# A Mamba block and a mixture of experts over 16 sequences: late weights behind the first spreads, four high parts on VectorE, pair sums on GpSimd in the last sequence, and new written orders at both ends

## The chip, the cores and the metric

The kernel runs on one core of a Trainium2 chip. The metric is the device time of one execution in microseconds. The same code also runs once under the hardware profiler, and all rows below are from that execution. The engines are called PE (matrix multiplication), DVE (VectorE), ACT (ScalarE), POOL (GpSimd) and SP (SyncE, which here only issues DMAs). Each works through its own list of instructions in order and waits for the others at semaphores.

## The reference, cut to what matters

The input `x` is 16 sequences of 512 tokens with 128 channels, in fp32. Two residual blocks follow each other:

```python
x = x + attn(layernorm(x))          # a selective scan, 256 inner channels, 16 states
x = x + ffn(layernorm(x))           # 8 experts, the best 2 of each token, and one shared expert

# attn
x_proj, z = split(x @ W_in + b_in)
u = silu(x_proj)
B, C = split(u @ W_xproj + b_xproj)            # 16 values each per token
dt = softplus(u @ W_dt + b_dt)
# for each token t, channel d, state s:
h[d, s] = h[d, s] * exp(dt[t, d] * A[d, s]) + dt[t, d] * u[t, d] * B[t, s]
y[t, d] = sum over s of h[d, s] * C[t, s] + D[d] * u[t, d]
out = (y * silu(z)) @ W_out + b_out

# ffn
h = silu(x @ w1.T) * (x @ w3.T);  out_e = h @ w2.T        # for each of the 9 experts
out = sum over e of out_e * weight[e] + shared
```

## The kernel before

One sequence is one unit of work. Its 512 tokens lie along the free dimension, and the 256 inner channels are two halves `c` of 128 partitions. A *step* `a` is one half and one state, so there are 32 steps to a sequence, 0 to 15 for the first half. The names in the orders are tasks, `name.argument+sequence`:

- `x_t`, `xp`, `z`, `bc`, `dl` (PE) transpose and project the normalised input; `x_tc`, `u`, `zs`, `bcc`, `dlc` (ACT) take the results out of PSUM. `dlc` gives `dt`, `bcc` the rows of B and C.
- `rows` and `spread` (SP) write B and C to DRAM and read them back, copied to all 128 partitions, into `b_all` and `c_all`, in four groups of four states. In the first sequence `bs` and `cs` issue B and C of a group apart. Each is 1024 KB.
- `w` makes `dt * u`. `dbu` (POOL, line 785) multiplies it by B for four steps at once. `decay` (ACT, line 689) makes exp(dt * A) of a step in one of two PSUM banks.
- `scan` (DVE, line 902) runs the recurrence of a step over 512 tokens. For the steps in `by_dve(m)` it writes back into PSUM, and `mul` (DVE, line 910) multiplies by C into `hc`. For all others it writes to `hc`, and `hcp` (POOL, line 795) multiplies two neighbours by C in place. `hc` has four slots, `dbu` eight.
- `red` (PE, line 1079) adds one step to `y_acc`: four transposing matmuls, which free the slot in `hc`. `ycopy`, `gy`, `gyc`, `proj`, `projc` finish the first block.
- `mom2`, `agg2`, `rs2`, `norm2`, `split`, `splitc`, `xhi`, `xlo` normalise the result and split it into a high and a low part. `route`, `routec`, `rexp`, `rank` choose the experts. `h1` and `h3` (PE, line 989, three matmuls for each of 18 units, two units to an expert), `silu` (ACT), `g` (DVE), `eo` (PE, line 996, the output of one expert), `sc` (ACT) and `comb` (DVE) do the second block. `shared` is the shared expert's output. `store` writes the sequence.
- `whi` and `wlo` split the nine expert weights into high and low parts once, at the start. `late` is six weight transfers (w_out, b_out, w2 of 1152 KB, the gate's weights and bias, a constant `below`) which `resb.0` (POOL, line 764), `proj.0` and later tasks wait for.

The order of each engine is written out by hand in three parts: `START` covers the beginning, `ORDER` is one window that is repeated with the sequence number going up by one, and `END` is the last stretch. The block of the experts lags the scan by two to three sequences. The two PSUM banks of `mixed` and the three of `h` are given out in the order of the PE list (`InTurn`), so a move of a PE task changes who waits for whom.

```python
START_TO, END_FROM = 3, SEQS - 1 - 1      # windows 4 to 13 are repeated, END covers the rest
```

In front of window 4 START has brought POOL to `w.0` of sequence 5. END has the rest of sequence 14 and all of 15.

Of the kernel before, what the change touches and what calls it, by code (L numbers as in the profile page):

```python
# [58 lines left out]
def by_pool(m):  # L59
# [51 lines left out]
        red.13+1 dl.0+2 dl.1+2 route.0 h1.2 red.14+1 red.15+1 h1.3 gy.0+1 red.16+1 h1.4 h1.5 red.17+1
        red.18+1 h1.6 red.19+1 bc.0+2 h3.2 eo.0 red.20+1 h3.3 red.21+1 red.22+1 h1.7 red.23+1 h1.8 h3.4
        red.24+1 red.25+1 eo.1 red.26+1 h3.5 red.27+1 red.28+1 red.29+1 h3.6 red.30+1 h1.9 red.31+1 gy.1+1
        eo.2 red.0+2 proj.0+1 z.0+2 h1.10 h1.11 red.1+2 red.2+2 z.1+2 h3.7 red.3+2 x_t.0+3 red.4+2 h1.12
        red.5+2 red.6+2 h3.8 eo.3 red.7+2 h3.9 xp.0+3 h1.13 red.8+2 red.9+2 h1.14 h3.10 h3.11 red.10+2
# [1038 lines left out]
```

## Time and profile before

| | us |
|---|---|
| runs (3) | 1208.53 median, 1208.41 to 1209.28 |
| profiled execution | 1208.65 |
| its span | 1206.8 |
| PE, DVE, ACT, POOL busy | 1125.5, 1092.8, 1091.0, 1048.5 |

The span runs from the first to the last instruction, and 1.85 us of the execution lie around it. Busy time is the time in which at least one instruction of an engine runs. The ends of matmuls are modelled, so PE can be shown busy over short gaps: how long a piece of PE work really takes is read from the distance between starts in the chain.

### The profile page before, as it was taken

How to read it: one execution, taken by the hardware profiler on the slowest of the kernel's cores; microseconds unless marked ns; L12 is line 12 of the kernel's file. 1: busy time of each engine (PE TensorE's matmuls, PEld its weight loads, DVE VectorE, ACT ScalarE, POOL GpSimd, SP SyncE). 2: the span in 40 equal slices, each digit the busy share in tenths (PEclk: the TensorE clock that was granted, in tenths of full speed). 3: DMA queues.
4: the chain of work that ended last, by engine and by line, in shares of the span. 5: the costliest groups of instructions: out<-in, count | busy, mean ns of one | idle time of the engine just before them, and what ended most of it. 6: DMA issues, size and time to landing. Idle time of an engine off the chain costs nothing.

```text
span 1206.8 us, 21930 instructions
## 1 busy us (share of the span) xinstructions
PE 1125.5 (93%) x7352; PEld 949.5 (79%) x7352; DVE 1092.8 (91%) x1666; ACT 1091.0 (90%) x1916; POOL 1048.5 (87%) x459
## 2 busy tenths in 40 slices
...
GB/s 239 223 209 82 142 157 117 183 38 262 19 282 24 203 100 82 219 18 281 27 212 88 127 182 12 288 18 250 50 163 146 64 236 10 182 118 1 19 9 10
DMA packets 49456, 153.68 MB, mean 127 GB/s; under 512 B 4416, under 2 KB 31424, under 8 KB 32832
## 3 DMA queue, kind: packets, MB, share of 16 engines
...
q8 instruction: 59, 0.97, 0.3%
...
## 4 chain that ended last, share of the span: by engine, by line
POOL 45%; PE 27%; issue 15%; ACT 6%; DVE 4%; DMA 1%; SPq 1%; POOLq 0%; DVEq 0%; ACTq 0%
POOL dbu L785 23%; POOL hc L795 18%; PE h L989 12%; PE mixed L996 8%; PE y_acc L1079 4%; DVE hc L902 2%; ACT da L689 2%; POOL res L764 1%; POOL w_s L772 1%; ACT L689 1%; DMA below<-in_below 1%; POOL rstd L756 1%; DVE g L951 1%; PE mixed L989 1%; ACT silu L723 1%
## 5 line engine op out<-in xcount | busy, mean ns | idle before, releaser
L785 POOL TENSOR_TENSOR dbu<-w_s,b_all 128x2048 f32<-128x2048 f32 x128 | 585.8, 4577 | 19.9 <-DMA b_all<-bc_rows 19.9
L795 POOL TENSOR_TENSOR hc<-hc,c_all 128x1024 f32<-128x1024 f32 x151 | 359.2, 2382 | 51.7 <-DVE hc L902 51.2
L689 ACT ACTIVATE da<-dt_s,a_neg 128x512 f32<-128x512 f32 x512 | 346.0, 691 | 46.6 <-DVE hc L902 24.1
L902 DVE TENSOR_TENSOR_SCAN hc<-da,dbu 128x512 f32<-128x512 f32 x302 | 358.5, 1211 | 22.8 <-PE y_acc L1079 11.6
L1079 PE MATMUL y_acc<-ident,hc 128*128 128x128 f32 x2048 | 297.6, 282 | 43.3 <-POOL hc L795 30.7
L1079 PEld LDWEIGHTS y_acc<-ident,hc 128*128 128x128 f32 x2048 | 248.8, 145 | 97.8 <-POOL hc L795 41.1
L996 PEld LDWEIGHTS mixed<-w_s,g 128*128 128x128 f32 x2304 | 273.4, 193 | 26.0 <-DVE g L951 13.2
L996 PE MATMUL mixed<-w_s,g 128*128 128x128 f32 x2304 | 285.2, 277 | 8.9 <-DVE g L951 6.3
L902 DVE TENSOR_TENSOR_SCAN da<-da,dbu 128x512 f32<-128x512 f32 x210 | 252.7, 1218 | 16.0 <-POOL dbu L785 10.3
L989 PE MATMUL h<-x_hi,w_hi 128*128 128x512 f32 x576 | 257.5, 447 | 5.8 <-DVE g L951 4.3
L989 PE MATMUL h<-x_lo,w_hi 128*128 128x512 f32 x576 | 227.9, 396 | 0.0
L989 PE MATMUL h<-x_hi,w_lo 128*128 128x512 f32 x576 | 227.7, 395 | 0.0
L951 DVE TENSOR_TENSOR g<-silu,h 128x512 f32<-128x512 f32 x288 | 193.3, 676 | 28.2 <-PE h L989 14.4
L723 ACT ACTIVATE silu<-h 128x512 f32<-128x512 f32 x288 | 160.8, 602 | 13.9 <-PE h L989 9.9
L730 ACT ACTIVATE mixed<-mixed,comb 128x128 f32<-128x128 f32 x512 | 140.9, 339 | 23.3 <-PE mixed L996 18.6
L910 DVE TENSOR_TENSOR hc<-da,c_all 128x512 f32<-128x512 f32 x210 | 140.7, 680 | 5.8 <-PE y_acc L1079 4.8
L689 ACT ACT_TABLE_LOAD x111 | 142.4, 1283 | 2.0
L989 PEld LDWEIGHTS h<-x_hi,w_hi 128*128 128x128 f32 x576 | 109.2, 189 | 31.0 <-DVE g L951 8.2
L989 PEld LDWEIGHTS h<-x_hi,w_lo 128*128 128x128 f32 x576 | 108.5, 188 | 25.6
L989 PEld LDWEIGHTS h<-x_lo,w_hi 128*128 128x128 f32 x576 | 109.6, 190 | 9.9 <-issue 0.2
L723 ACT ACT_TABLE_LOAD x79 | 101.4, 1283 | 1.4
L959 DVE TENSOR_TENSOR acc<-mixed,acc 128x512 f32<-128x512 f32 x112 | 75.5, 674 | 10.8 <-ACT mixed L730 6.2
...
## 6 DMA issues: line engine op xcount, KB each, us to landing
b_all<-bc_rows SPq DMA_DIRECT2D x64, 1024.0 KB, 6.4
c_all<-bc_rows SPq DMA_DIRECT2D x64, 1024.0 KB, 8.8
...
```

The source lines that it names most:

```text
L689: act.activation(da[a % DA_SLOTS][:, :], dt_s[:, m % DT_SLOTS, c, :], ACT.Exp, scale=a_neg[:, a:a + 1]).then_inc(decay_made, 1)
L723: act.activation(silu[:, a % SILU_SLOTS, :], h_tile("h1", a, m)[:, :], ACT.Silu).then_inc(silu_made, 1)
L730: last = act.activation(block_, block_, ACT.Copy, scale=comb[:, b, a:a + 1])
L785: pool.tensor_tensor(dbu[:, at:at + AT_ONCE, :], w_s[:, c, None, :].broadcast_to([P, AT_ONCE, T]), b_all[:, s:s + AT_ONCE, :], ALU.mult).t ...
L795: pool.tensor_tensor(pair, pair, c_all[:, s:s + 2, :], ALU.mult).then_inc(c_by_pool, 1)
L902: dve.tensor_tensor_scan(dst, ring[:, :], dbu[:, a % DBU_SLOTS, :], 0.0, ALU.mult, ALU.add).then_inc(scanned, 1)
L910: dve.tensor_tensor(hc[:, a % HC_SLOTS, :], da[a % DA_SLOTS][:, :], c_all[:, s, :], ALU.mult).then_inc(c_by_dve, 1)
L951: dve.tensor_tensor(g[:, a % G_SLOTS, :], silu[:, a % SILU_SLOTS, :], h_tile("h3", a, m)[:, :], ALU.mult).then_inc(g_made, 1)
L959: dve.tensor_tensor(acc[:, :, :], as_blocks(tile), acc[:, :, :], ALU.add).then_inc(freed, 1)
L989: last = pe.matmul(dst[:, :], w, xx[:, :], start=(i == 0), stop=(i == 2))
L996: last = pe.matmul(as_blocks(tile)[:, b, :], g[:, slot, b * P:(b + 1) * P], w2_s[:, at:at + DM], start=(begins and b == 0 and f == 0), sto ...
L1079: last = pe.matmul(y_acc[:, b, :], hc[:, a % HC_SLOTS, b * P:(b + 1) * P], ident[:, :], is_transpose=True, start=(a % NS == 0 and b == 0), ...
```

## The change

1. SP, start: the late weights are issued behind all spreads of the first sequence, and B of groups 2 and 3 comes earlier. `loadres` of sequences 0 and 1 is moved too.
2. The high parts of the expert weights 1, 3, 5 and 7 are made on DVE instead of ACT. `w.1` of the first sequence is moved ahead of its scans.
3. `resb.0` on POOL goes from between `dbu.1` and `dbu.2` of the first sequence to behind `dbu.0` of the second. `dl.1` goes ahead of `z.1`, and `dlc.1` ahead of the first decays.
4. In the last sequence POOL adds each pair of products (`padd`, 16 times 128x512), and PE reduces only the sum: 16 `red` instead of 32. A `scan` or `mul` then waits for the reduction where its slot was an even one and for the add where it was an odd one (`hc_free`).
5. START and END are written anew for all engines, and END begins one window earlier, so it covers the rest of sequence 13 and all of 14 and 15. `ORDER` is unchanged.
6. Functions for "turned" steps come with it (`turned`, tasks `bt`, `wt`, `td`, `tb`, `btc`, `wtc`). Their list is empty and no order holds these tasks, so they issue nothing.

```diff
+HI_BY_DVE = [1,3,5,7]
+TURNED_FIRST = []
+PAIRED = 1
+def in_pairs(m):
+    return m >= SEQS - PAIRED
+def sums(m):
+    return range(0, STEPS, 2) if in_pairs(m) else range(STEPS)
+def sum_count(step, m):
+    return sum(len(sums(k)) for k in range(m)) + len([a for a in sums(m) if a <= step])
+def pair_count(step, m):
+    return STEPS // 2 * (m - (SEQS - PAIRED)) + step // 2 + 1
...
-START_TO, END_FROM = 3, SEQS - 1 - 1
+START_TO, END_FROM = 3, SEQS - 1 - 2
```

START on PE, first entries:

```diff
-        x_t.0 xp.0 xp.1 bc.0 dl.0 z.0 z.1 dl.1 red.0 red.1 red.2 red.3 x_t.0+1 red.4 red.5 red.6 red.7 red.8
+        x_t.0 xp.0 xp.1 bc.0 dl.0 z.0 dl.1 z.1 x_t.0+1 red.0 red.1 red.2 red.3 red.4 red.5 red.6 red.7
```

START on ACT, first entries:

```diff
-        aexp.0 x_tc.0 u.0 u.1 whi.0 whi.1 bcc.0 whi.2 whi.3 whi.4 whi.5 whi.6 whi.7 dlc.0 whi.8 decay.0
-        decay.1 zs.0 zs.1 dlc.1 decay.2 decay.3 decay.4 norm1.0+1 decay.5 decay.6 decay.7 decay.8 decay.9
+        aexp.0 x_tc.0 u.0 u.1 whi.0 bcc.0 dlc.0 whi.2 whi.4 dlc.1 zs.0 whi.6 decay.0 decay.1 whi.8 zs.1
+        decay.2 norm1.0+1 decay.3 x_tc.0+1 decay.4 decay.5 decay.6 decay.7 decay.8 decay.9 decay.10 decay.11
```

START on DVE, first entries and the place of `comb.0`:

```diff
-        mom1.0 agg1.0 winlo.0 norm1.0 x_lo.0 wlo.0 wlo.1 wlo.2 wlo.3 mom1.0+1 wlo.4 wlo.5 wlo.6 wlo.7
-        agg1.0+1 w.0 wlo.8 scan.0 mul.0 scan.1 mul.1 scan.2 mul.2 scan.3 mul.3 scan.4 mul.4 scan.5 mul.5
-        scan.6 scan.7 scan.8 mul.8 scan.9 mul.9 scan.10 scan.11 x_lo.0+1 w.1 scan.12 mul.12 scan.13 mul.13
+        mom1.0 agg1.0 winlo.0 norm1.0 x_lo.0 whi.1 whi.3 w.0 wlo.0 wlo.1 wlo.2 wlo.3 whi.5 mom1.0+1 agg1.0+1
+        wlo.4 whi.7 w.1 wlo.5 wlo.6 wlo.7 wlo.8 scan.0 mul.0 scan.1 mul.1 scan.2 mul.2 scan.3 mul.3 scan.4
+        mul.4 scan.5 mul.5 scan.6 scan.7 scan.8 scan.9 mul.8 mul.9 scan.10 scan.11 x_lo.0+1 scan.12 mul.12
...
-        scan.28+1 scan.29+1 mul.28+1 mul.29+1 comb.0 g.5 scan.30+1 scan.31+1 mul.30+1 mul.31+1 comb.1
+        mul.21+1 rank.7 scan.22+1 scan.23+1 comb.0 scan.24+1 scan.25+1 mul.24+1 mul.25+1 g.3 g.4 scan.26+1
```

START on POOL, first entries:

```diff
-        rs1.0 dbu.0 dbu.1 rs1.0+1 resb.0 dbu.2 hcp.6 dbu.3 hcp.10 dbu.4 hcp.14 dbu.5 hcp.18 dbu.6 hcp.22
-        dbu.7 w.0+1 hcp.26 dbu.0+1 rs1.0+2 dbu.1+1 hcp.2+1 dbu.2+1 rs2.0 hcp.6+1 dbu.3+1 w.1+1 hcp.10+1
+        rs1.0 dbu.0 rs1.0+1 dbu.1 dbu.2 hcp.6 dbu.3 hcp.10 dbu.4 hcp.14 dbu.5 hcp.18 dbu.6 hcp.22 dbu.7
+        w.0+1 hcp.26 dbu.0+1 rs1.0+2 resb.0 dbu.1+1 hcp.2+1 dbu.2+1 rs2.0 hcp.6+1 dbu.3+1 w.1+1 hcp.10+1
```

START on SP, first entries:

```diff
-        load.0 raw.0 load.0+1 rows.0 bs.0 bs.1 cs.0 loadres.0 late.0 cs.1 bs.2 cs.2 cs.3 bs.3 load.0+2
-        rows.0+1 spread.0+1 spread.1+1 spread.2+1 spread.3+1 load.0+3 rows.0+2 spread.0+2 spread.1+2
-        spread.2+2 loadres.0+1 spread.3+2 load.0+4 rows.0+3 spread.0+3 spread.1+3 spread.2+3 spread.3+3
+        load.0 raw.0 load.0+1 rows.0 bs.0 bs.1 cs.0 bs.2 cs.1 bs.3 cs.2 load.0+2 loadres.0 cs.3 late.0
+        rows.0+1 spread.0+1 spread.1+1 spread.2+1 spread.3+1 load.0+3 rows.0+2 loadres.0+1 spread.0+2
+        spread.1+2 spread.2+2 spread.3+2 load.0+4 rows.0+3 spread.0+3 spread.1+3 spread.2+3 spread.3+3
```

END on PE, from the first experts of sequence 13 to the first of sequence 15:

```diff
-        red.25-1 route.0-2 h1.0-2 red.26-1 h1.1-2 red.27-1 h1.2-2 red.28-1 h1.3-2 h3.0-2 h1.4-2 red.29-1
-        h1.5-2 shared.0-3 h1.6-2 h3.1-2 h3.2-2 red.30-1 red.31-1 h1.7-2 h3.3-2 eo.0-2 red.0 red.1 h1.8-2
-        h1.9-2 h3.4-2 h3.5-2 eo.1-2 red.2 red.3 h3.6-2 h3.7-2 eo.2-2 h1.10-2 gy.1-1 red.4 h1.11-2 red.5
...
-        h1.10-1 h3.8-1 red.26 h1.11-1 red.27 eo.3-1 h3.9-1 h1.12-1 red.28 z.1 h3.10-1 red.29 red.30 red.31
-        h1.13-1 h3.11-1 gy.1 eo.4-1 proj.0 h3.12-1 eo.5-1 h1.14-1 h3.13-1 h3.14-1 h1.15-1 eo.6-1 h1.16-1
-        h3.15-1 h1.17-1 split.0 h3.16-1 h3.17-1 eo.7-1 h1.0 h1.1 h3.0 route.0 shared.0-1 h1.2 h3.1 h3.2 h1.3
+        h1.17-3 h3.17-3 red.25-1 eo.7-3 h1.0-2 red.26-1 red.27-1 route.0-2 h3.0-2 h1.1-2 h1.2-2 h1.3-2
+        red.28-1 shared.0-3 red.29-1 h1.4-2 h1.5-2 h3.1-2 h3.2-2 red.30-1 red.31-1 h3.3-2 eo.0-2 h3.4-2
+        h1.6-2 eo.1-2 h3.5-2 red.0 h1.7-2 h1.8-2 red.2 h3.6-2 gy.1-1 eo.2-2 h3.7-2 h1.9-2 red.4 h3.8-2
+        proj.0-1 h3.9-2 eo.3-2 red.6 h1.10-2 h1.11-2 h1.12-2 eo.4-2 h1.13-2 h1.14-2 h1.15-2 h3.10-2 h3.11-2
+        h3.12-2 red.8 eo.5-2 h3.13-2 red.10 eo.6-2 h3.14-2 h1.16-2 z.0 h3.15-2 h1.17-2 split.0-1 red.12
...
+        h3.5-1 h3.6-1 red.22 red.24 eo.2-1 h3.7-1 h1.10-1 h3.8-1 h3.9-1 eo.3-1 h3.10-1 h1.11-1 red.26
+        h1.12-1 eo.4-1 h1.13-1 red.28 h1.14-1 z.1 h3.11-1 h3.12-1 red.30 h1.15-1 gy.1 h3.13-1 proj.0 eo.5-1
+        h3.14-1 h1.16-1 h3.15-1 eo.6-1 h3.16-1 split.0 h1.17-1 h3.17-1 eo.7-1 h1.0 route.0 h1.1 h3.0
```

END on DVE, the first steps of sequence 15 (new order only):

```diff
+        scan.31-1 rank.0-2 scan.0 rank.1-2 scan.1 rank.2-2 mul.0 rank.3-2 rank.4-2 rank.5-2 comb.7-3
+        rank.6-2 mul.1 g.1-2 g.2-2 scan.2 scan.3 rank.7-2 g.3-2 g.4-2 scan.4 comb.0-2 scan.5 g.5-2 mul.4
```

END on POOL, whole:

```diff
-        hcp.26-1 hcp.28-1 dbu.0 hcp.30-1 dbu.1 hcp.2 dbu.2 w.1 hcp.6 resb.0-1 dbu.3 hcp.10 dbu.4 rs2.0-1
-        hcp.12 hcp.14 dbu.5 hcp.18 dbu.6 hcp.22 dbu.7 hcp.26 hcp.28 resb.0 hcp.30 rs2.0
+        hcp.26-2 dbu.0-1 hcp.28-2 hcp.30-2 dbu.1-1 w.1-1 hcp.2-1 dbu.2-1 rs1.0 hcp.6-1 dbu.3-1 resb.0-2
+        hcp.10-1 dbu.4-1 hcp.12-1 hcp.14-1 dbu.5-1 hcp.18-1 dbu.6-1 rs2.0-2 hcp.22-1 dbu.7-1 w.0 hcp.26-1
+        dbu.0 hcp.28-1 hcp.30-1 w.1 dbu.1 padd.0 hcp.2 padd.2 dbu.2 padd.4 resb.0-1 hcp.6 padd.6 dbu.3
+        padd.8 hcp.10 rs2.0-1 padd.10 dbu.4 hcp.12 padd.12 hcp.14 padd.14 dbu.5 padd.16 hcp.18 padd.18 dbu.6
+        padd.20 hcp.22 padd.22 padd.24 dbu.7 hcp.26 padd.26 hcp.28 padd.28 hcp.30 padd.30 resb.0 rs2.0
```

The tasks:

```diff
+        def hc_free(a, m):
+            user, back = before(a, HC_SLOTS, STEPS)
+            if m < back:
+                return reduced, 0
+            if in_pairs(m - back) and user % 2:
+                return pair_added, pair_count(user, m - back)
+            return reduced, sum_count(user, m - back)
...
+                elif what == "whi":
+                    dve.wait_ge(raw_in[a // RAW], 16 * RAW)
+                    dve.tensor_copy(w13_hi[:, a * W13:(a + 1) * W13], stages[a]).then_inc(hi_by_dve, 1)
...
+                elif what == "padd":
+                    pool.wait_ge(*c_count(a + 1, m))
+                    at = a % HC_SLOTS
+                    pool.tensor_tensor(hc[:, at, :], hc[:, at, :], hc[:, at + 1, :], ALU.add).then_inc(pair_added, 1)
...
-                    pe.wait_ge(*c_count(a, m))
+                    if in_pairs(m):
+                        pe.wait_ge(pair_added, pair_count(a, m))
+                    else:
+                        pe.wait_ge(*c_count(a, m))
```

## Rows read from the trace of the kernel before

**Rows 1.** Profile page: busy time of all engines, costliest groups, DMA issues.
```profile
PE 1125.5 (93%) x7352; PEld 949.5 (79%) x7352; DVE 1092.8 (91%) x1666; ACT 1091.0 (90%) x1916; POOL 1048.5 (87%) x459
...
L795 POOL TENSOR_TENSOR hc<-hc,c_all 128x1024 f32<-128x1024 f32 x151 | 359.2, 2382 | 51.7 <-DVE hc L902 51.2
...
b_all<-bc_rows SPq DMA_DIRECT2D x64, 1024.0 KB, 6.4
```

**Rows 2.** Stretches: length, busy PE, PEld, DVE, ACT, POOL (count), clock, DMA share, GB/s.
```profile
0.00:50.00 50.00, 27.43 (x135) 19.01 (x136) 28.86 (x51) 29.61 (x44) 23.02 (x20) 0.74 0.76 279
50.00:100.00 50.00, 31.32 (x171) 25.02 (x169) 45.74 (x58) 35.45 (x49) 49.49 (x19) 0.81 0.42 170
...
600.00:700.00 100.00, 98.55 (x654) 82.50 (x653) 95.44 (x143) 97.60 (x176) 96.32 (x43) 1.00 0.41 157
...
1100.00:1150.00 50.00, 50.00 (x333) 44.13 (x332) 39.46 (x66) 38.40 (x75) 25.08 (x12) 1.00 0.04 12
```

**Rows 3.** Timeline of POOL: start, duration, instruction, idle before; one of sequence 14.
```profile
966.36 1.29 POOL L772 TENSOR_TENSOR w_s<-dt_s,u 128x512 f32<-128x512 f32 x1
```

**Rows 4.** Timeline of SP, which issues DMAs, first 30 us.
```profile
18.73 0.81 SPq L606 DMA_DIRECT2D b_all<-bc_rows  x2
...
21.76 0.44 SPq L588 DMA_DIRECT2D w_s<-in_w  x1
...
26.66 0.42 SPq L606 DMA_DIRECT2D b_all<-bc_rows  x1
```

**Rows 5.** Timeline of POOL in the first 60 us.
```profile
23.70 8.98 POOL L785 TENSOR_TENSOR dbu<-w_s,b_all 128x2048 f32<-128x2048 f32 x2 [15.79 <-DMA b_all<-bc_rows]
32.77 0.23 POOL L744 TENSOR_SCALAR minus_mean<-moments 128x4 f32<-128x4 f32 x1
...
36.19 1.27 POOL L764 TENSOR_TENSOR res<-res,bout_s 128x512 f32<-128x512 f32 x1 [1.48 <-DMA below<-in_below]
40.84 4.51 POOL L785 TENSOR_TENSOR dbu<-w_s,b_all 128x2048 f32<-128x2048 f32 x1 [3.38 <-DMA b_all<-bc_rows]
...
55.60 4.52 POOL L785 TENSOR_TENSOR dbu<-w_s,b_all 128x2048 f32<-128x2048 f32 x1
```

**Rows 6.** Timeline of DVE and, last row, of ACT in the first 50 us.
```profile
28.31 1.23 DVE L902 TENSOR_TENSOR_SCAN da<-da,dbu 128x512 f32<-128x512 f32 x1 [5.78 <-POOL dbu L785]
29.58 0.69 DVE L910 TENSOR_TENSOR hc<-da,c_all 128x512 f32<-128x512 f32 x1
...
34.29 1.23 DVE L902 TENSOR_TENSOR_SCAN da<-da,dbu 128x512 f32<-128x512 f32 x1 [2.16 <-ACT da L689]
...
41.75 2.33 DVE L902 TENSOR_TENSOR_SCAN hc<-da,dbu 128x512 f32<-128x512 f32 x2
45.45 1.23 DVE L902 TENSOR_TENSOR_SCAN da<-da,dbu 128x512 f32<-128x512 f32 x1 [1.37 <-POOL dbu L785]
...
31.57 0.69 ACT L667 ACTIVATE dt_s<-mixed,bdt_s 128x512 f32<-128x512 f32 x1
```

**Rows 7.** Timelines of SP and POOL: the `res` of sequence 1.
```profile
148.22 0.38 SPq L556 DMA_DIRECT2D res<-in_x  x1
...
158.32 1.27 POOL L764 TENSOR_TENSOR res<-res,bout_s 128x512 f32<-128x512 f32 x1 [1.36 <-DMA res<-in_x]
```

**Rows 8.** The chain that ended last: start, duration, piece; sequence 15.
```profile
1064.51 0.87 PE y_acc L1079 x8
1065.38 2.80 PE h L989 x12
1068.18 1.78 PE mixed L996 x16
...
1138.41 1.31 PE y_acc L1079 x12
...
1158.12 2.23 PE h L989 x9
```

**Rows 9.** Waits of POOL between 1052 and 1138 us: total, times, longest.
```profile
POOL hc L795 <- DVE hc L902: 18.2, 8, 5.5
```

**Rows 10.** Timeline of PE between 60 and 100 us.
```profile
84.27 5.33 PE L1079 MATMUL y_acc<-ident,hc 128*128 128x128 f32 x24 [4.68 <-POOL hc L795]
```

More of the change, by code:

```diff
@@ L52, with turned, dbu_count, turned_count @@
 ]
+TURNED_FIRST = []
+def turned(m):
+    return TURNED_FIRST[m] if m < len(TURNED_FIRST) else []
+def dbu_count(step, m):
+    own = [g for g in range(step // AT_ONCE + 1) if g not in turned(m)]
+    return sum(DBUS - len(turned(k)) for k in range(m)) + len(own)
+def turned_count(step, m):
+    own = [a for a in range(step + 1) if a // AT_ONCE in turned(m)]
+    return AT_ONCE * sum(len(turned(k)) for k in range(m)) + len(own)
+PAIRED = 1
[7 more added lines that the diff above has]
+    return STEPS // 2 * (m - (SEQS - PAIRED)) + step // 2 + 1
 def by_dve(m):
@@ L111 @@
[L111 to L115, printed above, removed]
@@ L178 @@
[L178 removed]
+        rs1.0 dbu.0 rs1.0+1 dbu.1 dbu.2 hcp.6 dbu.3 hcp.10 dbu.4 hcp.14 dbu.5 hcp.18 dbu.6 hcp.22 dbu.7
+        w.0+1 hcp.26 dbu.0+1 rs1.0+2 resb.0 dbu.1+1 hcp.2+1 dbu.2+1 rs2.0 hcp.6+1 dbu.3+1 w.1+1 hcp.10+1
+        dbu.4+1 hcp.14+1 dbu.5+1 hcp.18+1 dbu.6+1 hcp.22+1 dbu.7+1 hcp.26+1 w.0+2 dbu.0+2 dbu.1+2 rs1.0+3
+        w.1+2 resb.0+1 hcp.2+2 dbu.2+2 hcp.6+2 dbu.3+2 hcp.10+2 dbu.4+2 rs2.0+1 hcp.14+2 dbu.5+2 rs1.0+4
@@ L179 @@
+        hcp.18+2 dbu.6+2 hcp.22+2 dbu.7+2 w.0+3 hcp.26+2 dbu.0+3 hcp.30+2 dbu.1+3 hcp.2+3 w.1+3 dbu.2+3
+        hcp.6+3 dbu.3+3 resb.0+2 hcp.10+3 dbu.4+3 hcp.12+3 hcp.14+3 dbu.5+3 hcp.18+3 rs2.0+2 dbu.6+3
+        hcp.22+3 dbu.7+3 w.0+4 hcp.26+3 dbu.0+4 hcp.28+3 hcp.30+3 dbu.1+4 hcp.2+4 w.1+4 dbu.2+4 rs1.0+5
+        hcp.6+4 dbu.3+4 resb.0+3 hcp.10+4 dbu.4+4 hcp.12+4 hcp.14+4 dbu.5+4 rs2.0+3 hcp.18+4 dbu.6+4
         hcp.22+4 dbu.7+4 w.0+5
@@ L776, in task @@
                     c, s = step // NS, step % NS
-                    if s == 0:
+                    if not [g for g in range(c * NS // AT_ONCE, a) if g not in turned(m)]:
                         pool.wait_ge(w_made, NC * m + c + 1)
```

376 lines of the change are left out of this document (223 added, 153 removed).

## The prediction

> **What bounds the kernel now.** I read the page's first part [rows 1], then the busy time by stretch [rows 2], then the timelines of both ends, because those are what the change touches. In the middle PE is busy 98.6 of 100 us and POOL, ACT and DVE 96 to 98 of 100 [rows 2]: one sequence takes 69.4 us (POOL starts `w.0` of sequence 14 at 966.36, and this row recurs every 69.4 us, nine times from 342.02 on [rows 3]) and no engine has room. That stretch keeps its order, so what is gained before it is carried through it, and the question is what the two ends do. In the first 50 us POOL works 23 and DVE 29; in 1100 to 1150 PE is full and POOL works 25.1 [rows 2]. The start is therefore bound by data that arrives late and by the step loop of the first sequence, the end by PE.
>
> **First sequence, DMA order.** SP issues the first two B spreads at 18.73, then one C spread, then the late weights (`w2` at 21.76, 1152 KB), and only at 26.66 the B spread of group 2 (group 3 at 28.22, a row of the same form) [rows 4]. POOL ends `rs1` at 34.7, waits 1.48 us for the last late weight, does `resb.0` (1.27), waits 3.38 more for group 2 and starts `dbu.2` at 40.84 [rows 5]. The first spread lands at 23.70; from there to group 2's landing at 40.84 are 17.1 us for 5.7 MB (four spreads, `res`, the late weights), 3.0 us each [rows 4, 5]. With the late weights last, group 2 is the third megabyte behind the first and lands at 23.7 + 9 = 32.7. It stops being what `dbu.2` waits for; that is then scan 3, whose results free the slots. The old order also let DVE wait 2.16 us at 34.29 for a decay that stood on ACT behind `dlc.1`, done at 32.26 [rows 6]; the new one has PE do `dl.1` before `z.1` and ACT `dlc.1` before the decays, with `bc.0` and `dl.0` as early as before. Scan 0 stays where it is, 28.1 to 28.3: `dbu.0` waits for the first spread, not for DVE or ACT. Steps of scan and product take 1.87 us (34.29 to 41.75 for four), two bare scans 2.33 [rows 6]. Scan 3 ends at 28.2 + 3 x 1.87 + 1.2 = 35.0, `dbu.2` runs 35.0 to 39.5 (rs1, 2 us, and `dbu.1` are done at 34.7). Scan 7 ends at 28.2 + 6 x 1.87 + 2.34 = 41.8, where before scan 8 started at 45.45, behind `dbu.2`. `hcp.6` 41.8 to 44.1, `dbu.3` 44.1 to 48.6, `hcp.10` to 50.95, and `dbu.4` starts at 50.95 instead of 55.60 [rows 5]: **-4.65**.
>
> What moves with it: the four high parts on DVE. No row has an fp32 copy on DVE; below stands nothing, above 0.69 of a two-input operation of that size [rows 6]. I take 0.6, 2.4 in all, and cost it at nothing: before, DVE sat idle 5.78 us in front of scan 0 [rows 6]. If ACT's `whi.8` slips past 27, scan 0 slips with it, 0 to 1.5 us; that end is kept for the range. `w.1` moves from behind scan 11 to before scan 0, into the same idle. `resb.0` goes behind `dbu.0+1`, where POOL has no wait: **+1.25** [rows 5]. `loadres.0+1` now goes ahead of the spreads of sequence 2 instead of behind three of them: its `res` was issued at 148.22 and POOL waited 1.36 us for it at 158.32 [rows 7]: **-1.3**. It adds a wait: SP holds the next sequence's spreads until `comb.0` is done. In the new DVE order `comb.0` stands behind scan 23 instead of behind the product of step 29, and B has then 9 to 10 us of POOL work (`hcp.22`, `dbu.7`, `hcp.26`, `w.0`) to arrive in; a B spread's median is 6.4 [rows 1]. Nothing, or up to 3 us if it misses. The other moves in sequences 1 to 3 change places of equal work; POOL, DVE and ACT each wait some 5 us in 100 to 200, so I bound them by -3 and +3 and take 0. Start: **-4.7**.
>
> **Sequences 13 to 15, PE.** One h unit (three matmuls) is 0.70 us of the chain, one expert output 1.78, one reduction 0.44 [rows 8]. In the old order 12 h units and one output of sequence 13 are done when `red.0` of sequence 15 comes, in the new one 13 units and two outputs. The chain is PE there, so it comes **+2.5** later.
>
> **The last sequence.** Sixteen reductions go: 16 x 0.44 = 7.0 us of PE. Sixteen adds come to POOL. Nearest rows: POOL's `w` and `resb`, 512 elements with two inputs, 1.29 and 1.27 [rows 3, 5]; the lower bound is half a 1024-element product, 1.19 [rows 1], the upper 1.29. An operation of POOL starts some 0.03 to 0.05 before the one ahead of it ends in its row, so I take 1.25, 20.0 in all. From the first add to the last POOL has in its new order 6 `dbu` at 4.53, 10 products (`hcp`) at 2.33, 15 adds, one `resb`, one `rs2` (1.98): 27.2 + 23.3 + 18.8 + 1.25 + 2.0 = 72.5 us. Walking the orders against each other I find 2.7 us of waits: `hcp.2` for scan 3 behind two `g` (1.3), and about 1.4 at `red.8` and `red.26`, which the new order puts behind 8 us of PE work each while slots wait. 75.2, against 74.8 from the end of `red.0` (1064.95) to the end of `red.31` (1139.72) [rows 8]. So the adds go into POOL's waits (18.2 us in 1052 to 1138 [rows 9]) nearly whole, and the stretch stays: **+0.4**. But PE, which was its bound, is now idle in it by some 6 us and PE's saving is not the end's.
>
> The Trainium skill speaks against this step: the page "GPSIMD Engine Reference", section "4.1 Engine selection", sends elementwise adds on a tile to VectorE, GpSimd being about twice as slow. The trace agrees: 0.69 for a product on DVE against 1.19, half of 2.38, on POOL [rows 1, 6]. The page's figure for an add of 2048 fp32 elements, 4497 ns, would make an estimate of 1.12 each and 18.0 in all, and the end 2 us earlier.
>
> **The tail.** From `red.31` (1139.72) to h1.0 of the last sequence (1158.12) are 18.4 us [rows 8]. The bare durations of that path, each from its row in the timeline (ycopy 0.60, gy 0.44, gyc 0.69, proj 1.79, projc 0.69, bn_stats 0.87, aggregate 0.38, rs2 1.95, norm2 1.65, split 0.44, copy and high part 1.2, low part 0.69, and 14 handovers near 0.1) sum to 13; the rest is h units and outputs of sequence 14 standing ahead of it on PE. In the new order four units and one output of these are done before the last reduction, and 13.4 us of PE work are left ahead of h1.0. Between 13 and 18.4 I take 15: **-3.4**. Behind h1.0 nothing changes: 36 units, nine outputs, the last add and the store, 48.7 us.
>
> **Sum**, against the profiled execution of 1208.65 (span 1206.8 and 1.85 around it; the median of the runs, 1208.53, is 0.1 lower): -4.7 + 2.5 + 0.4 - 3.4 = -5.2, so **1203.4 us**.
>
> **Rivals.** (B) *PE stays the bound to the end.* If the new order of sequences 13 and 14 lets POOL start the last sequence earlier than PE work alone says, the last stretch ends with PE: the start's 4.7 and 7.0 of reductions, 1208.65 - 11.7 = **1197.0**. For it: the chain is PE without a gap from 1060 to 1200 [rows 8]; against: POOL's 72.5 us of work between first and last add, which no order shortens. (C) *The start's gain is given back* in sequences 1 to 3, because DVE is full from 50 us on (45.7 of 50 [rows 2]) and the spreads of sequence 2 now stand behind `comb.0`; or the late weights were hidden anyway behind scan 3. Then -0.5 is left, **1208.2**. Against: DVE's idle time in the first 50 us is what shrinks, and it counts like POOL's. (D) *The adds on POOL end late*, the case on the other side. Place: between `padd.0` and `padd.30`; price: every microsecond of the 18.2 us of waits that stays beside the 20.0 of adds [rows 9]. These waits are for scans, which wait for reductions to free slots, and the slot now comes free one operation later (product, add, reduction). My walk leaves 2.7; from 7.7 more on it is slower than before by over 0.2%; with 10 more **1213.4**. (E) *PE's clock falls in the new gaps.* Granted clock is 1.00 where no gap of PE is over half a microsecond and 0.81 in 50 to 100 us, where it waits 3.5 to 4.7 us between reductions; there 24 matmuls of a reduction take 5.33 us, twice the 2.6 of six at the end [rows 2, 8, 10]. My walk has one gap of 3.1 us before `red.2` and a few in the tail. If about 10 us of PE work on the path run at the 1.2 GHz level, that is +5: **1208.4**. The Trainium skill, "TensorE: Matmul & The Clock Gate", section "Part 1: The HAM clock gate", says likewise that idling brings the slower level back and activity releases it; the trace agrees with that. That the change doesn't do what it says has one form: the functions for turned steps come with it, but their list is empty, so they issue nothing.
>
> **Chances.** Forecast 0.48 (own range 1200 to 1206.5), B 0.20, C 0.15, D 0.10, E 0.07. What a measurement can tell from no change is 0.2%, 2.4 us. Faster than 1206.1: nearly all of the forecast (0.46), B, and a little of C and E: 0.67. Within 0.2%: 0.22. Slower: D and a remainder of the reordering that I bounded by +3: 0.11. The range of 8 in 10 takes in most of B and C and leaves D out: 1196 to 1209.5.
>
> **What would show it.** Start: `dbu.2` at about 35, `dbu.4` at about 51, `w.0` of sequence 4 near 268 (272.65 before), and no wait of POOL before a `res` add. C is right if that `w.0` is later than 271. End: PE idle several microseconds between the first and last reduction of sequence 15, and POOL busy in over 70 of some 75 us there; B if PE is without gaps, D if POOL waits over 10 us there, E if the granted clock is under 0.97 in any stretch behind 1050. The tail from the last reduction to the end of the span: 63.7 against 67.1. The forecast is wrong if the last reduction does not end near 1138, or if the tail stays at 67.

## The result and the profile after

The changed kernel takes 1207.66 us (median of 12 runs, 1204.9 to 1210.15), the kernel before 1209.75 (12 runs beside it, 1206.96 to 1212.33): ratio 0.9981, 95% interval 0.9972 to 0.9990. That is 2.3 us faster, where 5.2 were forecast. Its profiled execution spans 1206.4 us, against 1206.8.

The page of the changed kernel, and its stretches (columns as in [rows 2]):

```profile
PE 1123.4 (93%) x7288; PEld 944.6 (78%) x7288; DVE 1098.6 (91%) x1670; ACT 1090.9 (90%) x1914; POOL 1069.9 (89%) x475
```

```profile
0.00:50.00 50.00, 24.89 (x126) 17.75 (x127) 33.52 (x55) 26.46 (x38) 22.57 (x19) 0.72 0.76 276
50.00:100.00 50.00, 34.22 (x161) 26.69 (x160) 43.39 (x55) 36.59 (x50) 48.65 (x19) 0.67 0.43 173
...
1050.00:1100.00 50.00, 49.40 (x328) 43.54 (x327) 47.06 (x75) 47.94 (x90) 49.44 (x24) 1.00 0.34 124
1100.00:1150.00 50.00, 49.19 (x311) 41.57 (x310) 41.46 (x68) 43.46 (x78) 42.05 (x21) 1.00 0.04 12
```

POOL has 21 us more work (16 adds), TensorE 64 matmuls less. In the first 50 us DVE is *busier* by 4.7 us than before [rows 2], yet what came to it is 1.7 us of copies and `w.1` (0.7): something took longer. DVE's timeline of the changed kernel shows what:

```profile
20.75 0.69 DVE L1004 TENSOR_TENSOR w_s<-dt_s,u 128x512 f32<-128x512 f32 x1 [7.46 <-ACT dt_s L765]
21.36 2.49 DVE L991 TENSOR_TENSOR w_lo<-silu,w_hi 128x512 fp32r<-128x512 f32 x4
23.76 4.74 DVE L984 CAST w_hi<-silu 128x512 fp32r<-128x512 f32 x1
...
30.30 0.42 DVE L984 CAST w_hi<-g 128x512 fp32r<-128x512 f32 x1
30.64 0.69 DVE L1004 TENSOR_TENSOR w_s<-dt_s,u 128x512 f32<-128x512 f32 x1
...
31.84 1.89 DVE L991 TENSOR_TENSOR w_lo<-g,w_hi 128x512 fp32r<-128x512 f32 x3
33.66 1.22 DVE L1041 TENSOR_TENSOR_SCAN da<-da,dbu 128x512 f32<-128x512 f32 x1
```

The third high part takes 4.74 us, eleven times the fourth (0.42), and scan 0 starts at 33.66, 5.4 us later than before [rows 6]. POOL in the same stretch:

```profile
23.17 5.06 POOL L907 TENSOR_TENSOR dbu<-w_s,b_all 128x2048 f32<-128x2048 f32 x1 [15.54 <-DMA b_all<-bc_rows]
30.01 0.76 POOL L864 TENSOR_SCALAR minus_mean<-moments 128x4 f32<-128x4 f32 x1 [1.78 <-DVE moments L1025]
...
33.15 4.95 POOL L907 TENSOR_TENSOR dbu<-w_s,b_all 128x2048 f32<-128x2048 f32 x1
40.61 4.52 POOL L907 TENSOR_TENSOR dbu<-w_s,b_all 128x2048 f32<-128x2048 f32 x1 [2.51 <-DVE da L1041]
```

`dbu.0` runs from 23.17 to 28.23, the long high part from 23.76 to 28.50: it ends 0.3 us behind POOL's operation. `dbu.2` starts at 40.61 (forecast 35; 40.84 in [rows 5]), though it no longer waits for its spread but for scan 3. Where POOL starts sequence 4, and the ends of the last sequence (first and last add on POOL, then first and last reduction on PE):

```profile
278.34 1.29 POOL L894 TENSOR_TENSOR w_s<-dt_s,u 128x512 f32<-128x512 f32 x1
...
1066.21 1.30 POOL L923 TENSOR_TENSOR hc<-hc 128x512 f32<-128x512 f32 x1
...
1141.45 1.29 POOL L923 TENSOR_TENSOR hc<-hc 128x512 f32<-128x512 f32 x1
```

```profile
1070.97 0.60 PE L1231 MATMUL y_acc<-ident,hc 128*128 128x128 f32 x4
...
1142.80 0.66 PE L1231 MATMUL y_acc<-ident,hc 128*128 128x128 f32 x4
```

Four marks cut every profile into the forecast's terms: POOL's first `w` of sequence 4 (`w.0`), the start of `red.0` of sequence 15, the end of the last reduction, the end of the span. In us, with three kernels that are told below:

```
                       before   changed   e3       e11      e7
to w.0 of seq. 4       272.65   278.34    272.99   272.69   270.24
from there to red.0    791.69   792.63    792.93   792.78   792.62
red.0 to last red      75.38    72.49     72.54    76.92    72.57
last red to the end    67.08    62.94     62.94    62.91    62.87
```

Changed against before: +5.7, +0.9, -2.9, -4.1, in sum -0.4. Forecast: -4.7, +2.5, +0.4, -3.4. The spans are those of one profile each, and the first row moves most from one execution to the next: with the old start it lies between 272.65 and 272.99 in four profiles (before, e3, e11, e14), with the new one at 278.34 here and at 274.41 in e4.

### The profile page after: what moved, and what is told of

Read it like the earlier page. It is cut to its first block, busy times and chain, and to the rows that moved or that the text cites. A ratio compares the mean times of both kernels' runs of the same rounds, so it can differ in the third digit from the quotient of the medians.

```text
span 1206.4 us, 21820 instructions
## 1 busy us (share of the span) xinstructions
PE 1123.4 (93%) x7288; PEld 944.6 (78%) x7288; DVE 1098.6 (91%) x1670; ACT 1090.9 (90%) x1914; POOL 1069.9 (89%) x475
## 4 chain that ended last, share of the span: by engine, by line
POOL 47%; PE 22%; issue 16%; DVE 8%; ACT 7%; DMA 1%; DVEq 0%; POOLq 0%; ACTq 0%; SPq 0%
POOL dbu L907 23%; POOL hc L917 19%; PE h L1127 9%; PE mixed L1134 6%; PE y_acc L1231 4%; DVE hc L1041 4%; ACT da L810 2%; ACT L810 1%; POOL w_s L894 1%; POOL hc L923 1%; POOL res L884 1%; POOL rstd L876 1%; ACT silu L843 1%; DVE da L1041 1%; PE mixed L1198 1%
## 5 line engine op out<-in xcount | busy, mean ns | idle before, releaser
L1231 PE MATMUL y_acc<-ident,hc 128*128 128x128 f32 x1984 | 289.8, 282 | 36.3 <-POOL hc L917 23.3
L1231 PEld LDWEIGHTS y_acc<-ident,hc 128*128 128x128 f32 x1984 | 240.8, 145 | 93.6 <-POOL hc L917 37.2
```

The lines of the kernel that those rows point to most:

```text
L1231: last = pe.matmul(y_acc[:, b, :], hc[:, a % HC_SLOTS, b * P:(b + 1) * P], ident[:, :], is_transpose=True, start=(a % NS == 0 and b == 0), ...
```

## Experiments

All but e10 were timed in alternation with the kernel before, in three groups on one chip: e1 to e4; e7, e8, e9 and e11; e12, e13 and e14. e10 ran once, beside the last group. A ratio is to the kernel before, and a ratio times 1209.5 gives the microseconds.

**e3 and e4: one half of the change each.** e3 has `START_ORDER` of before and `HI_BY_DVE = []` in the changed kernel, e4 `END_ORDER`, `END_FROM` of before and `PAIRED = 0`.

```diff
-HI_BY_DVE = [1,3,5,7]
+HI_BY_DVE = []
```

> The first four windows in the order of the kernel before, all high parts on ScalarE; the last windows and the pair adds of the changed kernel. Theory (the new first part costs 5.7 us, the new last part gains 8): w.0 of sequence 4 at 272.6, the last sequence as in the changed kernel but 5.7 us earlier, about 1202.0 us, 7.8 below the kernel before. Rival 1 (the last part only gains because it takes back what the start lost, so that PE or GpSimd work sets its end): 1205 us or more. Rival 2 (as forecast, the last part is worth 0.5 us): 1209.

> The first windows of the changed kernel with its high parts on VectorE; the last windows and all 32 reductions of the kernel before. Theory: the start's loss of 5.7 us is carried to the end, 1209.75 + 5.7 = 1215.4 us, slower than before by 0.47%. Rival 1 (the loss is taken back in the last windows, whichever their order): 1210 to 1212 us. Rival 2 (the start did gain, as forecast): 1205.

e3: 1203.21 us, ratio 0.9951 (0.9939 to 0.9963). e4: 1212.43, 1.0033 (1.0022 to 1.0043). The new last part is worth -0.49% with the old start, and -0.52% with the new one (0.9981 against 1.0033): 5.9 to 6.3 us, not the 0.5 of the forecast and, as e3 shows, nothing that the start had lost first. The new start costs 0.33% with the old end and 0.30% with the new: 3.6 to 4.0 us, where 4.7 of gain were forecast. The expected 5.7 came from one profile; in e4's the same start has `w.0` of sequence 4 at 274.41, 1.8 us behind before, and the span ends 1.7 behind (1208.5), so nothing of the loss is taken back in the last windows.

**e1 and e2: the long high part.** e1 makes the four high parts by a two-input operation, e2 puts all four ahead of `w.0`.

```diff
-dve.tensor_copy(w13_hi[:, a * W13:(a + 1) * W13], stages[a])
+dve.tensor_tensor(w13_hi[:, a * W13:(a + 1) * W13], stages[a], stages[a], ALU.max)
```

```diff
-whi.1 whi.3 w.0 wlo.0 wlo.1 wlo.2 wlo.3 whi.5 mom1.0+1 agg1.0+1 wlo.4 whi.7 w.1
+whi.1 whi.3 whi.5 whi.7 w.0 wlo.0 wlo.1 wlo.2 wlo.3 mom1.0+1 agg1.0+1 wlo.4 w.1
```

> The four high parts stay on VectorE at their places, but each is made by a two-input maximum of the tile with itself in place of a copy; the values are the same. Theory (a copy of an fp32 tile on VectorE is held for as long as a GpSimd operation runs beside it: whi.5 took 4.74 us and ended 0.27 behind dbu.0): the two-input form takes about 0.69 us each, whi.5 too, and scan 0 starts at about 29.6 instead of 33.66 (the 5.16 us of work behind whi.5 counted from 23.76 + 0.69). That lead is carried: w.0 of sequence 4 near 274.3 instead of 278.34, and about 1203.7 us against 1207.7. Rival 1 (whi.5 was late for another reason, its data or ScalarE): it still ends near 28.5, nothing changes. Rival 2 (the start is lost by the orders of sequences 1 to 3 and not by the high part): scan 0 comes earlier, but w.0 of sequence 4 stays within 1 us of 278.3 and the time within 1.5 us of 1207.7.

> whi.5 and whi.7 stand on VectorE directly behind whi.3, in its idle time of 7.5 us ahead of w.0, where GpSimd does nothing. Theory: both take 0.43 us as whi.1 and whi.3 do, scan 0 starts at about 28.5 (33.66 less 4.74 less 0.42, and dbu.0 ends at 28.2), w.0 of sequence 4 near 273.2, and 1202.5 us. Rival 1 (another reason than GpSimd holds whi.5): it is long there too and w.0 slips behind 20.75. Rival 2 (orders of sequences 1 to 3): scan 0 early, w.0 of sequence 4 still within 1 us of 278.3, time within 1.5 us of 1207.7.

e1: 1211.26, ratio 1.0021 (1.0012 to 1.0031), slower than the changed kernel. e2: 1206.68, 0.9981 (0.9971 to 0.9991), no better. My first theory, that only a copy is held, is wrong. DVE of e1:

```profile
22.53 0.68 DVE L984 TENSOR_TENSOR w_hi<-silu 128x512 fp32r<-128x512 f32 x1
...
24.44 4.07 DVE L991 TENSOR_TENSOR w_lo<-silu,w_hi 128x512 fp32r<-128x512 f32 x1
...
30.23 6.18 DVE L991 TENSOR_TENSOR w_lo<-g,w_hi 128x512 fp32r<-128x512 f32 x3
36.34 1.22 DVE L1041 TENSOR_TENSOR_SCAN da<-da,dbu 128x512 f32<-128x512 f32 x1
```

and of e2:

```profile
22.39 4.65 DVE L991 TENSOR_TENSOR w_lo<-silu,w_hi 128x512 fp32r<-128x512 f32 x1
...
29.97 1.22 DVE L1041 TENSOR_TENSOR_SCAN da<-da,dbu 128x512 f32<-128x512 f32 x1
```

Now a low part is held: whatever operation with both inputs in SBUF comes to DVE first while `dbu.0` runs (23.43 to 27.95 in e1, 21.96 to 26.49 in e2) ends 0.55 us behind it. e1 has a second one beside `dbu.1` (three low parts in 6.18 us, the last of them 4.98). e2's scan 0 is 3.7 us earlier than the changed kernel's and `w.0` of sequence 1 as well (78.67 against 82.36), yet its time is the same. In its profile the lead is still 3.2 us at `w.0` of sequence 3 (208.27 against 211.44) and gone at sequence 4 (278.54); between 210 and 220 the granted clock is 0.66 there, 1.00 in the changed kernel. But that is one of its slower executions (1209.04, median 1206.68), so why the lead is missing in the time of all twelve stays open.

**e10: the low parts alone.** The kernel before with one order edited:

```diff
-wlo.0 wlo.1 wlo.2 wlo.3 mom1.0+1 wlo.4 wlo.5 wlo.6 wlo.7 agg1.0+1 w.0 wlo.8 scan.0
+wlo.0 mom1.0+1 agg1.0+1 w.0 wlo.1 wlo.2 wlo.3 wlo.4 wlo.5 wlo.6 wlo.7 wlo.8 scan.0
```

> The kernel before with one edit: VectorE's low parts 1 to 8 stand behind w.0 and not ahead of it. Without any hold they end near 26.8, ahead of dbu.0's end at 28.2, and scan 0 stays at 28.3. Theory of the hold (two SBUF inputs on VectorE wait for a GpSimd operation under way): dbu.0 starts at 23.7, after four of them; the fifth takes about 4 us in place of 0.69 and ends with dbu.0, three more follow, and scan 0 starts at 30.1. Since scan 2 waits for its decay until 34.29 anyway, both expect the time of before, within 1 us.

One run: 1213.19 us against 1208.77 (nine runs, none above 1210.55), and `w.0` of sequence 4 at 277.27, 4.6 later. DVE of e10, then POOL:

```profile
21.81 11.70 DVE L857 TENSOR_TENSOR w_lo<-silu,w_hi 128x512 fp32r<-128x512 f32 x5
33.44 1.88 DVE L857 TENSOR_TENSOR w_lo<-g,w_hi 128x512 fp32r<-128x512 f32 x3
35.24 1.22 DVE L902 TENSOR_TENSOR_SCAN da<-da,dbu 128x512 f32<-128x512 f32 x1
```

```profile
23.47 9.50 POOL L785 TENSOR_TENSOR dbu<-w_s,b_all 128x2048 f32<-128x2048 f32 x2 [15.65 <-DMA b_all<-bc_rows]
...
42.19 4.52 POOL L785 TENSOR_TENSOR dbu<-w_s,b_all 128x2048 f32<-128x2048 f32 x1 [4.76 <-DVE da L902]
```

The first row holds five low parts. Two of these and the two `dbu`, by source line for what runs after 28 us (shortest/median/longest in ns, first and last start):

```profile
L857 DVE TENSOR_TENSOR w_lo<-silu,w_hi x2: 4981/4988/4995, 23.6 to 28.5; 128x512 fp32r<-128x512 f32 x2
L785 POOL TENSOR_TENSOR dbu<-w_s,b_all x2: 4596/4771/4946, 23.5 to 28.0; 128x2048 f32<-128x2048 f32 x2
```

Three low parts took 0.68, and the fourth and the fifth 5.0 us each: one was held beside `dbu.0`, was let through at its end, and the next one came to DVE when `dbu.1` had begun and was held for that. Each ended 0.5 us behind its `dbu`. The hold was as expected, but it came twice, and scan 0 starts at 35.24 instead of the expected 30.1, which also makes the "same time" wrong.

**e7: nothing left to be held.** The changed kernel, with DVE's low parts 0 to 7 and all high parts ahead of `w.0`, and on ACT `whi.2 whi.4 whi.6` ahead of `dlc.0` and `whi.8` ahead of `dlc.1`:

```diff
-whi.1 whi.3 w.0 wlo.0 wlo.1 wlo.2 wlo.3 whi.5 mom1.0+1 agg1.0+1 wlo.4 whi.7 w.1 wlo.5 wlo.6 wlo.7 wlo.8 scan.0
+whi.1 whi.3 wlo.0 wlo.1 whi.5 wlo.2 wlo.3 whi.7 wlo.4 wlo.5 wlo.6 wlo.7 w.0 wlo.8 mom1.0+1 agg1.0+1 w.1 scan.0
```

> The changed kernel; in its first sequence VectorE does all four high parts and the low parts 0 to 7 ahead of w.0, in its idle time, ScalarE does whi.2, 4 and 6 ahead of dlc.0, and only wlo.8, the statistics and w.1 are left between w.0 and scan 0. Theory (VectorE operations with two SBUF inputs are held for the rest of dbu.0, and all that stands behind the held one comes after it): with one or none left, scan 0 starts 0.1 to 0.7 us behind the end of dbu.0, at 26.6 to 28.6, instead of 5.4, 3.5 and 3.8 us behind it; w.0 of sequence 1 at 76.5 (82.36, 78.67 and 80.09 in the three kernels with this start), w.0 of sequence 4 at 272.5, and 1203.8 us (1207.7 less 3.9). Rival (the place of scan 0 is not what sets the first sequence; its DMAs or slots do): w.0 of sequence 1 not earlier than 78.5 and 1206.5 us or more.

1200.26 us, ratio 0.9935 (0.9913 to 0.9957): 7.9 us faster than before and 5.6 faster than the changed kernel (the two intervals lie apart), by the order of a dozen instructions. The expectation was 3.9 faster than the changed kernel, with `w.0` of sequence 4 at 272.5 and not at 270.24; the 1.7 us above it lie within the intervals. DVE and POOL of e7:

```profile
22.04 0.66 DVE L1004 TENSOR_TENSOR w_s<-dt_s,u 128x512 f32<-128x512 f32 x1
27.18 1.23 DVE L1041 TENSOR_TENSOR_SCAN da<-da,dbu 128x512 f32<-128x512 f32 x1 [4.48 <-POOL dbu L907]
```

```profile
22.42 4.65 POOL L907 TENSOR_TENSOR dbu<-w_s,b_all 128x2048 f32<-128x2048 f32 x1 [14.53 <-DMA b_all<-bc_rows]
...
34.15 4.52 POOL L907 TENSOR_TENSOR dbu<-w_s,b_all 128x2048 f32<-128x2048 f32 x1 [0.59 <-DVE da L1041]
...
49.87 4.56 POOL L907 TENSOR_TENSOR dbu<-w_s,b_all 128x2048 f32<-128x2048 f32 x1
```

Scan 0 waits for `dbu.0` and nothing else, `dbu.2` and `dbu.4` start at 34.15 and 49.87 (forecast 35 and 50.95), and `w.0` of sequence 1 at 75.91, 4.7 us ahead of before. This is the start that the prediction described, but for scan 0: it comes 1.0 us earlier than forecast, because the first spread lands earlier (`dbu.0` at 22.42, 23.70 in [rows 5]).

**e8, e9, e12: the other parts of the start**, each with the new last part. e8 is e3 with the late weights behind the last C spread and `resb.0` later:

```diff
-bs.0 bs.1 cs.0 loadres.0 late.0 cs.1 bs.2 cs.2 cs.3 bs.3 load.0+2
+bs.0 bs.1 cs.0 bs.2 cs.1 bs.3 cs.2 cs.3 loadres.0 late.0 load.0+2
```

e9 adds `dl.1` ahead of `z.1`, `dlc.1` ahead of `zs.0` and `w.1` ahead of scan 0. e12 is e9 with the high and low parts of e7 in it and `rs1` of sequence 1 ahead of `dbu.1`, as in the change; its sequences 1 to 3 keep the old order.

> The old order of the first windows with the last part of the changed kernel (1203.2 us); from the change's first sequence only the order of DMAs (late weights behind the last C spread) and resb.0 behind dbu.0 of sequence 1. Theory of the prediction: dbu.2 no longer waits for its spread but for scan 3 and starts at 37.3 instead of 39.77, dbu.4 at about 51.5 instead of 54.92, resb.0 adds 1.25 later where GpSimd is full, so w.0 of sequence 4 at 270.8 instead of 272.99 and 1201.0 us. Rival (what the spreads gain is taken back in sequences 1 to 3, whose order is the old one): 1203 us.

> The kernel of e8 with the second dt moved as in the change: dl.1 ahead of z.1, dlc.1 ahead of zs.0 and the decays, w.1 on VectorE ahead of scan 0. Scan 2 then waits for nothing (2.31 us before) unless decay.2 is later than 31.8. Theory: scan 0 at 28.5 (w.1 is held until dbu.0 ends), dbu.2 at 35.3, dbu.4 at 50.9, w.0 of sequence 4 at 270, 1200 us. Rival: w.1 beside dbu.0 and one more change of ScalarE's function in the start cost what the 2.31 us give, 1201 to 1202 us.

> The first sequence of e7 (all low parts but one and all high parts ahead of w.0, late weights last, second dt early), sequences 1 to 3 in the old order with resb.0 behind dbu.0 of sequence 1, the new last part. Between w.0 of sequence 1 and w.0 of sequence 4 the new order took 194.3 to 196.0 us (e7, e4, e1, the changed kernel), the old one 192.0 to 193.4 with resb.0 in it (before, e3, e8, e9). Theory (the new order of sequences 1 to 3 itself costs 1 to 3 us): w.0 of sequence 1 at 75.9, of sequence 4 at 269.3, and 1199.4 us against 1200.3 of e7. Rival (an earlier first sequence is swallowed in sequences 1 to 3 under either order): w.0 of sequence 4 at 270.2 or later, 1200.3 us or more.

e8: 1203.14 (0.9948, 0.9931 to 0.9964); e9: 1202.55 (0.9943, 0.9922 to 0.9962); e12: 1200.22 (0.9932, 0.9918 to 0.9946). In e8 `dbu.2` starts at 37.57 as worked out, but `dbu.4` at 53.77 (expected 51.5), `w.0` of sequence 1 at 79.75, where e11 has it with the old start, and that of sequence 4 at 272.93, as in e3: the DMA order with the moved `resb.0` is worth nothing. In e9 `w.0` of sequence 1 is at 78.48 and that of sequence 4 at 271.90 (expected 270), and its time is nearer to its rival; `w.1`, held beside `dbu.0`, took 2.81 us. e12 is no faster than e7 (`w.0` of sequence 1 at 75.31, of sequence 4 at 269.47, 194.2 us between them; 194.3 in e7, 192.0 before). The time can't tell its theory (1199.4) from its rival (1200.3), but the stretch between the marks speaks for the rival: with either order, 2 of the 4.7 to 5.3 us won in the first sequence are gone by sequence 4. The moved `resb.0` is 1.27 us of POOL's work in that stretch; e8, which has it, loses 0.6 there against e3.

**e13: the `res` load ahead of the spreads**, alone in the kernel before.

```diff
-spread.0+2 spread.1+2 spread.2+2 loadres.0+1 spread.3+2
+loadres.0+1 spread.0+2 spread.1+2 spread.2+2 spread.3+2
```

> The kernel before with one edit in SP's order: the res load of sequence 1 stands ahead of the spreads of sequence 2 instead of behind three of them. The prediction's term: GpSimd's wait of 1.36 us for it at 158.32 goes, 1.3 us earlier from there on, 1208.0 against 1209.3. Rival: the wait goes, but GpSimd then waits as long for scans or the spreads, 1209.3.

1215.11, ratio 1.0045 (1.0031 to 1.0060): both expectations wrong. SP of e13, then POOL:

```profile
146.86 0.39 SPq L556 DMA_DIRECT2D res<-in_x  x1
147.57 0.34 SPq L606 DMA_DIRECT2D b_all<-bc_rows  x1
```

```profile
152.26 4.51 POOL L785 TENSOR_TENSOR dbu<-w_s,b_all 128x2048 f32<-128x2048 f32 x1 [5.66 <-issue]
```

The load waits on SP for `comb.0` (its last operation on DVE ends at 146.76) until 146.86 and the spreads behind it start 7.9 us later than before (139.72). In the changed kernel `comb.0` stands six scans earlier in DVE's order, the load goes at 138.29 and the first spread at 139.01: there the wait has its cover, and e13 shows it gone where the SP edit stands alone. The move of `comb.0` alone was not run.

**e11 and e14: the adds.** e11 is e3 with all 32 reductions and no adds; e14 is the kernel before with the adds and 16 reductions, in the old order.

```diff
-red.0 h1.7-2 h1.8-2 red.2
+red.0 red.1 h1.7-2 h1.8-2 red.2 red.3
```

```diff
-hcp.30-1 dbu.1 hcp.2 dbu.2 w.1 hcp.6
+hcp.30-1 dbu.1 padd.0 hcp.2 padd.2 dbu.2 padd.4 w.1 hcp.6 padd.6
```

> The old start with the new order of the last windows, but all 32 reductions of the last sequence on TensorE and no adds on GpSimd: each second reduction stands right behind the first of its pair. Against 1203.2 us with the adds. Theory (TensorE is busy 49.2 to 49.4 of 50 us from 1050 to 1150 with the adds and would have to take 16 reductions of 0.44 us more): 7 us later less what is idle, 1209 us, which is about the kernel before; the gain of the last part is then that of the adds. Rival (the gain is the new order's and the adds only move work from TensorE to GpSimd, whose 20 us of adds lie in waits): 1203 to 1204 us. Rival 2 (GpSimd is the bound of the last sequence with the adds): 1198 to 1201 us.

> The kernel before with the pair adds alone: old start, old order of the last windows, in the last sequence 16 reductions and 16 adds on GpSimd behind each pair's product. Theory (adds and new order are worth their gains each by itself: e11 against e3 gave 4.0 us for the adds, e11 against before 2.1 for the order): 1205.2 us. Rival 1 (in the old order GpSimd starts the last sequence later and TensorE is the bound, so 16 reductions of 0.44 us come off in full): 1202.3. Rival 2 (the old order leaves GpSimd's waits for scans in place, 18.2 us, and the adds come on top): 1209 us or more.

e11: 1207.24, 0.9987 (0.9977 to 0.9998). e14: 1226.39, 1.0147 (1.0131 to 1.0163). In the new order the adds bring 0.36%, 4.4 us, all of it between `red.0` and the last reduction (76.9 against 72.5 us in the table). In the old order they cost 17.8 us. POOL's waits from 1050 to 1160 in e14, then those of the changed kernel from 1051 to 1144:

```profile
POOL hc L895 <- DVE hc L1020: 10.9, 2, 7.2
POOL hc L889 <- DVE hc L1013: 4.6, 3, 3.9
```

```profile
POOL hc L917 <- DVE hc L1041: 1.1, 2, 1.0
POOL hc L923 <- DVE hc L1048: 0.3, 1, 0.3
```

In e14 an add (L895) stands in POOL's queue ahead of the next `dbu` and waits up to 7.2 us for a product of DVE, in whose queue `g` operations stand ahead and wait up to 3.0 us each for TensorE's `h`; TensorE in its turn waits 15.7 us for POOL at its reductions (busy 39.8 of 50 us from 1100 on, granted clock 0.91). The prediction's rival D is real under the old order: the adds are as good as the order around them, and the theory that the two parts add up is refuted.

## Why the prediction was wrong, point by point

**The step that failed: "the four high parts on DVE", taken as 2.4 us and "cost ... at nothing", in 5.78 us of idle time ahead of scan 0.** Most of that time is idle because POOL works on `dbu.0` (23.70 to 28.2), and in these traces a copy from SBUF to SBUF or an operation with two SBUF inputs that comes to DVE meanwhile ends only 0.3 to 0.6 us behind POOL's. I looked at the high parts only; the new order also puts five of the nine low parts behind `w.0`, and those count the same. What is held costs little itself, but what stands behind it comes after `dbu.0`: scan 0 starts 5.4 us behind the end of `dbu.0` in the changed kernel, 3.5 in e2, 7.2 behind it in e10, and 0.1 in e7. The trace of before had the hint in two rows, the same operation ahead of POOL's work and beside it (DVE, `w.0` and `w.1`; the second ends 0.5 us behind POOL's `dbu.3`, 48.34 to 52.87):

```profile
21.28 0.66 DVE L870 TENSOR_TENSOR w_s<-dt_s,u 128x512 f32<-128x512 f32 x1
...
52.02 1.41 DVE L870 TENSOR_TENSOR w_s<-dt_s,u 128x512 f32<-128x512 f32 x1
```

The Trainium skill states the rule, "SBUF — State Buffer", section "SBUF: two separate sides": VectorE and GpSimd share a pair of ports as an exclusive lock, which an operation of VectorE in a 2-port mode or with two SBUF inputs needs, and the other side blocks. The traces agree (4.74, 4.07, 4.65 and twice 5.0 us in place of 0.43 and 0.68). I had weighed another rule of the skill and left out this one, which spoke against the change.

**"Scan 0 stays where it is, 28.1 to 28.3"**: 33.66, and 27.18 once the hold is gone. The risk that the prediction did price, ACT's `whi.8` slipping past 27, came true (28.67), but DVE reached the low part that needs it only at 33.05.

**"Start: -4.7"**: with the hold gone the first sequence gave 4.7 (e7), partly by luck: `dbu.4` was 5.7 us earlier, 1.0 of it from an earlier first spread that the forecast did not have, and 1.0 was lost again before `w.0` of sequence 1. At sequence 4 the gain is 2.4. If `resb.0` costs its whole 1.25 there, which no run shows alone, it was set against 1.3 from the `res` load, and that gain does not show in the balance, though POOL no longer waits there; the other 1 us goes in sequences 1 to 3, whose exchanged places I bounded by 3 us and took as 0. So even without the hold the start is worth some 2 to 3 us (e7 against e3: 1.9 by the ratios, whose intervals overlap, 2.7 by the mark), not 4.7. Rival C's test (`w.0` of sequence 4 later than 271) is met by the changed kernel, but by a loss, not by a gain given back.

**"Sequences 13 to 15, PE: +2.5"**: +0.9 in the changed kernel, +1.2 in e3 and +1.1 in e11. TensorE is busy for 197.5 of the 200 us from 850 to 1050 before and after, so the missing 1.5 us are not waits; open.

**"That stretch stays: +0.4"**: -2.9. POOL's part came out to the tenth, with some luck: from the end of the first add (1067.51) to that of the last (1142.74) are 75.2 us, POOL is busy for 72.7 of them (72.5 forecast), the adds took 1.27 to 1.30 each in their rows, and of 18.2 us of waits [rows 9] 1.4 are left (2.7 forecast); the rest are short gaps. But I let `red.0` follow the first add at once. TensorE starts it at 1070.97, 3.5 us behind, because in its new order two outputs and four units stand between the last reduction of sequence 14 and it. The last reduction does follow the last add. POOL's stretch and TensorE's overlap instead of coinciding, and 75.2 was measured on the wrong engine. The prediction also had TensorE idle for some 6 us in this stretch. Its stretch between first and last reduction, before and in the changed kernel (columns as in [rows 2]):

```profile
1064.34:1139.72 75.38, 75.34 (x509) 66.70 (x508) 66.97 (x100) 67.96 (x127) 56.20 (x23) 1.00 0.11 39
```

```profile
1070.97:1143.46 72.49, 71.45 (x453) 61.38 (x452) 65.62 (x98) 69.75 (x130) 70.15 (x36) 1.00 0.04 12
```

It is idle for 1.0 us: 3.9 us of its work left the stretch and 1.0 came back as idle time. TensorE still nearly sets this stretch, which is closer to rival B than to the forecast. By the table the new order alone makes it 1.5 us longer (e11) and the adds 4.4 shorter (e3 against e11), of the 7.0 us of reductions that they save.

**"The tail: -3.4"**: -4.1, 62.9 us against 63.7 forecast, the same in all four kernels with the new order. In PE's new order 8 h units and three outputs stand between the last reduction and h1.0 of the last sequence (in the chain below the row at 1157.68), where the old one had 12 and four: 14.2 us against 18.4, forecast 15. From h1.0 to the end are 48.7 us, as forecast.

```profile
1142.80 0.66 PE y_acc L1231 x4
1143.46 0.69 PE h L1127 x3
...
1144.23 0.64 PE mixed L1120 x4
...
1144.90 0.70 DVE sz L1056
...
1145.65 2.05 PE mixed L1206 x16
1147.70 1.79 PE mixed L1134 x16
...
1157.68 0.82 PE h L1127 x3
```

The end as a whole: -0.5 forecast, -6 measured, close to the 7.0 us of reductions of rival B, but made up otherwise: +0.9 of work ahead, -2.9 and -4.1, the last of them from the new order alone (62.9 in e11 too). Rival E is out for the changed kernel (granted clock 1.00 in every stretch behind 1050). So two errors of opposite sign, some 8.5 us at the start (-4.7 forecast, +3.8 measured) and 5.6 at the end, left a miss of 3 us; the time alone would have shown neither.
